# One transformer layer on one core: the prologue worked by halves of the first tile

## The reference

```python
mod = (silu(c) @ wmod).reshape(8, 6, 1, 128)       # sa, ca, ga, sb, cb, gb
h = layernorm(x) * (1 + ca) + sa
q, k, v = einsum('bsx,xAnh->Abnsh', h, w)          # 16 heads of 64; q += q_bias
emb = einsum('sf,fnh->nsh', sinusoids, positional) # relative positions
a = (q @ k.T + relative_causal(q @ emb.T)) * 64 ** -0.5
o = softmax(where(causal, a, -1e9)) @ v
x = x + ga * (o @ out_kernel + out_bias)
h = layernorm(x) * (1 + cb) + sb
x = x + gb * moe(h)      # 16 experts, argmax gate, 256 places each, 128 -> 512 -> 128
```

## Time and profile before

| | |
|---|---|
| median of 3 runs | 873.09 us (872.3 to 876.68) |
| the profiled execution's own time | 866.77 us |
| its span, first to last instruction | 864.9 us |
| PE busy in the span | 850.2 us, 98% |
| ACT, DVE, POOL busy | 84%, 76%, 62% |
| first x loads issued (ACT, SP); third load on ACT's queue | 0.72 us; 1.65 us |
| first score matmul starts | 17.86 us after the span's start |
| steps 0, 1, 2 last | 10.38, 13.09, 12.38 us |
| mean granted TensorE clock | 0.996 of full speed |

### The profile page before, as it was taken

How to read it: one execution, slowest core, us unless ns; L and a number is a source line. 1 busy time by engine, 2 the same in 40 slices (tenths; PEclk the granted TensorE clock), 3 DMA queues, 4 the chain that set the end, 5 groups by cost and what they waited for, 6 DMA issues and landing times.

```text
span 864.9 us, 17642 instructions
## 1 busy us (share of the span) xinstructions
PE 850.2 (98%) x5584; PEld 683.2 (79%) x5584; DVE 659.1 (76%) x2041; ACT 726.7 (84%) x2014; POOL 539.6 (62%) x797
## 2 busy tenths in 40 slices
PE   8999999999999999999999999999999999999996
PEld 6778777787777887778877788777887777877996
DVE  5878778887878778777878688777878767877574
ACT  5988889888888888888889888888988898885663
POOL 3655565666657766766576765776567755673465
PEclk9999999999999999999999999999999999999999
DMA  8000990000000100000000000000000000006781
GB/s 296 2 1 2 234 230 14 13 20 19 14 13 1 38 2 13 13 19 19 13 13 2 28 1 13 13 11 12 13 14 7 18 13 11 4 17 195 252 262 41
DMA packets 25468, 41.41 MB, mean 48 GB/s; under 512 B 3318, under 2 KB 17511, under 8 KB 24992
## 3 DMA queue, kind: packets, MB, share of 16 engines
q1 hardware_dynamic: 21728, 33.60, 13.1%
q0 software_dynamic: 3072, 5.94, 1.9%
q10 hardware_dynamic: 576, 0.75, 0.3%
HBM read 25.93 MB, written 16.82 MB: 49 GB/s over the span
## 4 chain that ended last, share of the span: by engine, by line
PE 92%; DVE 1%; DMA 1%; ACT 1%; issue 1%; POOL 0%; POOLq 0%; SPq 0%; DVEq 0%
PE bank L906 23%; PE bank L939 17%; PE bank L867 16%; PE bank L919 16%; PE bank L946 5%; PE bank L891 5%; PE bank L903 3%; PE bank L1206 3%; PE bank L1181 2%; DMA x<-xbuf 1%; ACT prob L640 0%; PE bank L1172 0%; PE bank L850 0%; PE bank L954 0%; PE bank L975 0%
## 5 line engine op out<-in xcount | busy, mean ns | idle before, releaser
L468 POOL TENSOR_SCALAR prob<-prob,rsum 128x128 f32<-128x128 f32 x508 | 263.0, 536 | 226.1 <-DVE rsum L1341 220.9
L640 ACT ACTIVATE prob<-srow,nmax 128x512 f32<-128x512 f32 (+3 forms) x512 | 285.9, 559 | 56.5 <-DVE nmax L1329 55.1
L1329 DVE CUSTOM_DVE_ANT_0 srow<-bank,consts 128x512 f32<-128x512 f32 (+3 forms) x512 | 247.0, 489 | 50.5 <-issue 38.5
L919 PE MATMUL bank<-consts,prob 128*128 128x128 f32 x1280 | 201.7, 272 | 0.4 <-ACT pt L649 0.4
L919 PEld LDWEIGHTS bank<-consts,prob 128*128 128x128 f32 x1280 | 158.1, 141 | 23.7 <-ACT pt L649 1.7
L649 ACT ACTIVATE pt<-bank 128x384 f32<-128x384 f32 x318 | 157.0, 498 | 10.6 <-PE bank L919 10.5
L1346 DVE SCALAR_TENSOR_TENSOR qx<-bank,qbias,consts 128x512 f32<-128x512 f32 x128 | 96.0, 750 | 72.9 <-PE bank L867 70.3
L939 PE MATMUL bank<-pt,v 128*64 128x512 f32 x1008 | 149.6, 439 | 0.2
L906 PE MATMUL bank<-khi,qhi 128*128 128x512 f32 (+2 forms) x384 | 140.4, 366 | 0.6 <-DVE nmax L1329 0.4
L461 POOL TENSOR_TENSOR qlo<-qx,qhi 128x384 fp32r<-128x384 f32 x128 | 129.3, 1010 | 13.8 <-ACT qhi L605 8.3
L906 PE MATMUL bank<-khi,qlo 128*128 128x512 f32 (+2 forms) x384 | 130.2, 339 | 0.0
(11 more groups left out here) (229 smaller groups left out, 1420.5 us busy)
## 6 DMA issues: line engine op xcount, KB each, us to landing
xbuf<-fill SPq DMA_DIRECT2D x4, 1540.0 KB, 24.0
x<-xbuf SPq DMA_DIRECT2D x13, 385.0 KB, 4.4
raw<-in_w SPq DMA_DIRECT2D x16, 256.0 KB, 10.1
prob<-in_w SPq DMA_DIRECT2D x16, 256.0 KB, 4.6
h2T<-in_xt SPq DMA_DIRECT2D x8, 256.0 KB, 2.7
out<-row SPq DMA_DIRECT2D x8, 256.0 KB, 2.3
x<-in_x SPq DMA_DIRECT2D x1, 1792.0 KB, 12.7
modb<-mod_rows SPq DMA_DIRECT2D x1, 1536.0 KB, 7.3
```

The lines of the kernel that those rows point to most:

```text
L468: end = gp.tensor_scalar(part, part, rsum[:, par, 4 * h + q:4 * h + q + 1], 1.0, ALU.mult, ALU.mult)
L640: act.activation(prob[:, par, h, QOFF[q]:QOFF[q] + P * (q + 1)], srow[:, k % 4, 0:P * (q + 1)], ACT.Exp, bias=nmax[:, par, k:k + 1], scale ...
L919: last = pe.transpose(out[:, n * P:(n + 1) * P], prob[:, par, h, QOFF[q] + k * P:QOFF[q] + (k + 1) * P], ident)
L1329: dve.tensor_tensor_reduce(out=srow[:, k % 4, 0:w], in0=scb[k % 2][:, 0:w], in1=mask[:, S - w:S], scale=-1.0, scalar=BIG, op0=ALU.add, op1 ...
```

## The change

- **Loads.** The two halves of the first x tile count on semaphores of their own. On ACT's queue the modulation weights go ahead of pair 0's weights; on SP's the table of query factors (`consts`) goes ahead of the sinusoids. The load of all other x is cut into batch 1 and the rest, which comes after the output weights.
- **First tile.** Statistics, root, x-hat and transposes are done for row tiles 2 and 3 first, then for 0 and 1. The first modulation columns are read by ACT. Modulation is computed twice, to fp32 by DVE and straight to the high part by ACT, half by half. The low parts of pair 0's weights move from DVE to POOL, and half of the sinusoids' low part too.
- **First products.** Keys come first, and the six products that need no low part of the input are mixed with those that do. The second modulation columns and rows come after them. The low part of the last query tile is made by DVE, that of the others by POOL.
- **First values.** The first four value tiles, and the one of step 1, are one plain fp32 matmul each, from `hn` and the raw weights. The split of the value weights moves from the prologue (high part on ACT, low part on POOL) to POOL in step 1.
- **Tables and casts.** The tables of pairs 1 to 3 move into step 0, those of pairs 4 to 7 into step 1. The casts of the weights of pairs 1 to 3 move from ACT to POOL.
- **Batch 1.** Its statistics move from block 0 of step 1 to blocks 6 and 7 of step 0, its x-hat from step 1 to blocks 0 and 1 of step 2. The copy of the modulation rows moves from step 1 to block 5 of step 0.
- **Idle matmuls.** 36 of 128 columns become 10 of 512; 20, 8 and 6 others are gone, 4 are new.

```diff
-    into = scb[1] if a0 == 0 else trb[i]
+    into = (scb[1] if a0 == 0 else trb[0], opb)[i]
...
-    sp.dma_start(h2T[HD:P, :], ktab_d).then_inc(s["ktab"], 16)
...
+    sp.dma_start(h2T[HD:P, :], ktab_d).then_inc(s["ktab"], 16)
...
-    sp.dma_start(x[:, QT:TILES, :], x_d[:, QT:TILES, :]).then_inc(s["x1"], 16)
+    sp.dma_start(x[:, QT:2 * QT, :], x_d[:, QT:2 * QT, :]).then_inc(s["x1"], 16)
...
+    sp.dma_start(x[:, 2 * QT:TILES, :], x_d[:, 2 * QT:TILES, :]).then_inc(s["xr"], 16)
...
-    root(0, 1, True)
+    gp.wait_ge(s["va0"], 1)
+    gp.tensor_tensor(rstd[:, 0, 2:QT], vare[:, 0, 2:QT], mhalf[:, 2:QT], ALU.pow).then_inc(s["rs0"], 1)
+    gp.wait_ge(s["va1"], 1)
+    gp.tensor_tensor(rstd[:, 0, 0:2], vare[:, 0, 0:2], mhalf[:, 0:2], ALU.pow).then_inc(s["rs1"], 1)
+    heads = lambda t: t[:, 0, 0:2 * P].rearrange("p (h c) -> p h c", h=2)[:, :, 0:HD]
+    gp.wait_ge(s["fhi"], 1)
+    gp.tensor_tensor(heads(wlo), wall[:, 0, 0:P].rearrange("p (h d) -> p h d", h=2), heads(whi),
+                     ALU.subtract).then_inc(s["flp"], 1)
+    gp.wait_ge(s["fhi"], 2)
+    gp.tensor_tensor(wlo[:, 0, 2 * P:3 * P], wall[:, 0, P:2 * P], whi[:, 0, 2 * P:3 * P], ALU.subtract)\
+        .then_inc(s["flp"], 1)
+    def high_w(a0, a1):
+        for h in range(2):
+            gp.tensor_copy(whi[q_cols(a0, a1, h)], wall[q_raw(a0, a1, h)]).then_inc(s["whp"], 1)
+        gp.tensor_copy(whi[:, a0:a1, 2 * P:3 * P], wall[:, a0:a1, P:2 * P]).then_inc(s["whp"], 1)
...
-    def low_wv():
+    def split_wv():
...
+        gp.wait_ge(s["w_v"], 16)
+        gp.tensor_copy(wvhi[:, :], wv).then_inc(s["wv"], 1)
...
-            low_q(j, 1)
+            if j > 0:
+                low_q(j, 1)
+            if first and a == 1:
+                split_wv()
...
+    waits(gp, ("kt", 2), ("flp", 2))
+    gp.tensor_tensor(klo[HD:P, 1, :], h2T[HD:P, :], khi[HD:P, 1, :], ALU.subtract).then_inc(s["klp"], 1)
+    waits(gp, ("klp", 1), ("qh", 1))
+    gp.tensor_tensor(qlo[:, 0, 0:2 * P], qx[:, 0, P:3 * P], qhi[:, 0, 0:2 * P], ALU.subtract)\
+        .then_inc(s["ql"], 1)
+    gp.wait_ge(s["wall1"], 16)
+    high_w(1, 4)
+    low_q(0, 1)
...
-    low_q(0, 0)
-    low_wk(1, 4, 3)
-    low_wv()
+    low_wk(1, 4, "whp", 3)
...
-    act.dma_start(x[:, 2:QT, :], x_d[:, 2:QT, :]).then_inc(s["x0"], 16)
-    act.dma_start(wall[:, 0:1, :], wall_d[:, 0:1, :]).then_inc(s["wall0"], 16)
+    act.dma_start(x[:, 2:QT, :], x_d[:, 2:QT, :]).then_inc(s["x0b"], 16)
...
+    act.dma_start(wall[:, 0:1, :], wall_d[:, 0:1, :]).then_inc(s["wall0"], 16)
...
-    bias_g(0, 1, 2)
+    act.wait_ge(s["mod_mm"], 1)
+    act.activation(modT[:, 0, :], bank[0][:, 0:B], ACT.Copy).then_inc(s["modT"], 1)
+    act.activation(modT[:, 1, :], bank[0][:, B:2 * B], ACT.Copy, bias=1.0).then_inc(s["modT"], 1)
+    def first_high():
+        act.wait_ge(s["t_x0"], 1)
+        act.wait_ge(s["modT"], 2)
+        act.activation(vhi[:, 2 * P:S], opb[:, 2 * P:S], ACT.Identity, bias=modT[:, 0, 0:1],
+                       scale=modT[:, 1, 0:1]).then_inc(s["vh0"], 1)
+        act.wait_ge(s["hn0"], 1)
+        act.activation(vhi[:, 0:2 * P], prb[0][:, 0:2 * P], ACT.Identity, bias=modT[:, 0, 0:1],
+                       scale=modT[:, 1, 0:1]).then_inc(s["vhi"], 1)
...
+        if k == 1:
+            high_g(1, 4, 3, "whi")
...
-            bias_g(1, PAIRS, 4)
-        if k == 3:
-            high_g(4, PAIRS, 5, "whi")
-        if k == 4:
-            act.wait_ge(s["wall2"], 16)
+            bias_g(1, 4, 4)
...
+        if k == 3:
+            high_g(4, PAIRS, 5, "whi")
+        if k == 4:
+            bias_g(4, PAIRS, 6)
+        if k == 5:
+            act.wait_ge(s["wall2"], 16)
...
+    first_high()
+    bias_g(0, 1, 2)
...
-    act.wait_ge(s["modT"], 2)
-    normed(0, opb)
-    high(0)
-    act.wait_ge(s["wall1"], 16)
-    high_wq(1, 4, 0)
-    high_wq(1, 4, 1)
-    high_wk(1, 4)
-    high_wv()
+    evac_k(0, 0, opb)
...
-    evac_k(0, 0)
-    evac_k(0, 1)
-    high_g(1, 4, 3, "whi")
+    evac_k(0, 1, opb)
...
-    pe.wait_ge(s["zero"], 2)
-    idle(36)
+    def idle_wide(n):
+        for _ in range(n):
+            pe.matmul(prb[0][:, :].rearrange("p (t c) -> p t c", t=QT), ones16[:, :],
+                      ones16[:, None, :].to_broadcast([P, QT, P]), start=True, stop=True)
+    pe.wait_ge(s["zero"], 1)
+    idle_wide(10)
...
-    pe.wait_ge(s["small"], 16)
-    b_table(0, 1)
...
-    idle(20)
...
-    turn_x(0, opb)
+    pe.wait_ge(s["xn0"], 1)
+    for q in (2, 3):
+        last = pe.transpose(opb[:, q * P:(q + 1) * P], xn[:, q, :], ident)
+    last.then_inc(s["t_x0"], 1)
+    pe.wait_ge(s["xn"], 1)
+    for q in (0, 1):
+        last = pe.transpose(prb[0][:, q * P:(q + 1) * P], xn[:, q, :], ident)
+    last.then_inc(s["t_x"], 1)
+    pe.wait_ge(s["small"], 16)
+    b_table(0, 1)
+    idle(4, trb[0])
+    def first_products():
+        k_of = lambda w, x_, i: pe.matmul(opb[:, :], w[:, 0, 2 * P:3 * P], x_, start=(i == 0), stop=(i == 2))
+        q_of = lambda h, w, x_, i: pe.matmul(prb[h][:, :], w[:, 0, h * P:(h + 1) * P], x_,
+                                             start=(i == 0), stop=(i == 2))
+        pe.wait_ge(s["fhi"], 3)
+        pe.wait_ge(s["flp"], 2)
+        pe.wait_ge(s["flo"], 1)
+        pe.wait_ge(s["hn"], 1)
+        pe.wait_ge(s["vhi"], 1)
+        k_of(whi, vhi[:, :], 0)
+        k_of(wlo, vhi[:, :], 1)
+        q_of(0, whi, vhi[:, :], 0)
+        pe.wait_ge(s["vlo"], 1)
+        k_of(whi, vlo[:, :], 2).then_inc(s["kp"], 1)
+        q_of(0, wlo, vhi[:, :], 1)
+        q_of(0, whi, vlo[:, :], 2).then_inc(s["qp"], 1)
+        pe.wait_ge(s["bias"], 2)
+        q_of(1, whi, vhi[:, :], 0)
+        q_of(1, wlo, vhi[:, :], 1)
+        q_of(1, whi, vlo[:, :], 2).then_inc(s["qp"], 1)
+    first_products()
...
-    idle(8)
...
+    def plain_v(out, g, t):
+        pe.matmul(out[:, :], hn[:, t * P:(t + 1) * P], wv[:, g * S:(g + 1) * S], start=True, stop=True)\
+            .then_inc(s["vp"], 1)
...
-        if k % QT == 0:
+        if j == 0 and k == 0:
+            pe.wait_ge(s["ql0"], 1)
+        elif k % QT == 0 or (j == 0 and k == 1):
...
-        if k == 2:
-            pe.wait_ge(s["modT"], 3)
-            w_table(4, PAIRS)
+        if k == 0:
+            pe.wait_ge(s["wall1"], 16)
+            w_table(1, 4)
+        if k == 1:
+            b_table(1, 4)
...
-            pe.wait_ge(s["wv"], 2)
+            pe.wait_ge(s["w_v"], 16)
...
-            pe.wait_ge(s["whi"], 5)
-            pe.wait_ge(s["wlo"], 2)
+            pe.wait_ge(s["modR"], 1)
...
-            project_v(V_INTO[k - 4], *V_FIRST[k - 4])
+            plain_v(V_INTO[k - 4], *V_FIRST[k - 4])
+    def second_step(k):
+        if k == 1:
+            pe.wait_ge(s["wall2"], 16)
+            pe.wait_ge(s["ve"], 1)
+            w_table(4, PAIRS)
+        if k == 2:
+            pe.wait_ge(s["bias"], 3)
+            b_table(4, PAIRS)
...
-                project_v(prb[1], *V_OF[a][1:])
+                if first and a == 2:
+                    pe.wait_ge(s["wv"], 2)
+                if first and a == 1:
+                    plain_v(prb[1], *V_OF[a][1:])
+                else:
+                    project_v(prb[1], *V_OF[a][1:])
+            if first and a == 1:
+                second_step(k)
...
-    pe.wait_ge(s["fhi"], 3)
-    pe.wait_ge(s["flo"], 3)
-    project_q(0, None, 0, 0)
-    project_q(0, None, 0, 1)
-    project_k(0, None, 0)
-    pe.wait_ge(s["wall1"], 16)
-    w_table(1, 4)
-    pe.wait_ge(s["wall2"], 16)
-    b_table(1, PAIRS)
-    pe.wait_ge(s["hn"], 1)
-    idle(6, opb)
...
+    dve.memset(ones16[:, :], 1.0).then_inc(s["zero"], 1)
...
-    dve.memset(ones16[:, :], 1.0).then_inc(s["zero"], 1)
...
-    dve.wait_ge(s["x0"], 32)
...
+    def first_stats(q0, landed, done, moments, ready):
+        dve.wait_ge(s[landed], 16)
+        for q in (q0, q0 + 1):
+            end = stats_of(0, q, x_of(0, q))
+        end.then_inc(s[done], 1)
+        dve.wait_ge(s[done], 1)
+        for q in (q0, q0 + 1):
+            end = dve.bn_aggr(mom[:, 0, q, :], stats[:, 0, q, :])
+        end.then_inc(s[moments], 1)
+        dve.wait_ge(s[moments], 1)
+        dve.tensor_scalar(vare[:, 0, q0:q0 + 2], mom[:, 0, q0:q0 + 2, 1], EPS, None, ALU.add)\
+            .then_inc(s[ready], 1)
+    def first_xhat(q0, ready, done):
+        dve.wait_ge(s[ready], 1)
+        for q in (q0, q0 + 1):
+            end = dve.tensor_scalar(xn[:, q, :], x_of(0, q), mom[:, 0, q, 0:1], rstd[:, 0, q:q + 1],
+                                    ALU.subtract, ALU.mult)
+        end.then_inc(s[done], 1)
+    first_stats(2, "x0b", "st0", "rst0", "va0")
+    first_stats(0, "x0", "st1", "rst1", "va1")
+    dve.wait_ge(s["e_silu"], 1)
...
-    dve.wait_ge(s["fhi"], 1)
-    heads = lambda t: t[:, 0, 0:2 * P].rearrange("p (h c) -> p h c", h=2)[:, :, 0:HD]
-    dve.tensor_tensor(heads(wlo), wall[:, 0, 0:P].rearrange("p (h d) -> p h d", h=2), heads(whi),
-                      ALU.subtract).then_inc(s["flo"], 1)
-    dve.wait_ge(s["fhi"], 2)
...
-    xhat1(0)
```

(69 more changed lines are left out.)

83 lines of the change are left out of this document (41 added, 42 removed).

## The result

The changed kernel took 877.53 us (median of 20 runs, 874.9 to 880.12), the kernel before 873.20 us beside it (20 runs, 871.94 to 876.96). The ratio is 1.0043, with a 95% interval of 1.0033 to 1.0053.

What follows compares the result with a forecast made beforehand. PE, busy for 98% of an 864.9 us span, was taken as the bound. Start -3.8, step 0 +2.75, step 1 -0.2, step 2 +0.2 sum to -1.05: 873.09 becomes 872.0 us; own range 870.5 to 873.5, whole 867.8 to 875.2.

Steps and rivals of the forecast that it cites:

- The start of the first scores: Prologue: first scores at 14.1 us instead of 17.86, -3.8 us, ends -5.3 and -2.0.
- the other branch: Prologue, beside PE's products and modulation: query evacuation, high part and low parts of keys and query, arriving at 13.9 us.
- the low clock lasts: Third rival: all nine products and modulation at clock 0.50, start 15.9, sum +0.8, 873.9 us; chance 0.13.
- Step 0, first half: First to fifth block: third maximum waits behind the table's cast and low part, fifth block at +5.15, so +1.55 us.
- Step 0, second half: Plain value tiles +0.76 and statistics with aggregates +0.66, instead of a wait of 0.25: +1.2 us.
- a wait that was there: End of step 0: a wait of 0.25 us before the change, set against the half's added costs.
- Step 1: Statistics go, tables, biases and one plain tile come (1.75 us): -0.2 us, ends -0.5 and +0.9.
- Loses its wait for the statistics: Step 1: ACT gets 0.6 + 0.18 us more on 11.85 busy, but no longer waits for the statistics.
- Step 2: Two pairs of x-hats delay the third maximum: +0.2 us, ends 0 and +0.8.
- 1.4 of 1.3 free: Step 2: the x-hats delay the third maximum by 1.4 us where 1.3 is free, giving +0.2.
- POOL's casts: Rival: POOL's casts hold the projection of pair 1, beside DVE done at 23.0, +3.0, 875.0 us; chance 0.15.
- count in full: Rival: the start's gain counts in full, step 0 costs only +0.8 to +1, total 867.8 to 869.6 us; chance 0.22.

Runs made afterwards that it cites:

- the filled prologue: Changed kernel with more 512-column multiplications of ones in the prologue (twelve instead of ten, more behind the table, modulation and transposes); ratio 1.0018 to the kernel before.
- columns later: Changed kernel with the low table part of pairs 1 to 3 and the late modulation columns moved later in step 0; ratio 1.0031 to the kernel before.
- statistics later: Changed kernel with batch 1's statistics and aggregate back at the start of step 1; ratio 1.0043 to the kernel before.
- the kernel before, filled: Kernel before with 41 instead of 20 multiplications of ones between the modulation's first part and the transposes; ratio 0.9994 to the kernel before.

## Why the prediction was wrong

*The start of the first scores* (-3.8, range -5.3 to -2.0; measured -2.55). Statistics, roots, x-hats, modulation and low part came as worked out (10.34 against 10.3); the x-hats took 1.53 beside POOL, where I had put 1.11 + 0.8, and a root of two columns 0.73, where I had taken 1.05. The step that failed is "I take the lower clock for the first three or four products and the full one after". All nine ran at 0.50, until 14.1 us, and the filled prologue showed its price, 1.95 us. It also showed that the other branch, which I had at 13.9, is done by 13.36. I had counted the ones-matmuls that the change takes out of PE's prologue and had the rival "the low clock lasts" for it, at 0.13. That was too little: the only row I had of the lower clock followed one idle stretch of 1.37 us. In the changed kernel the fall came 3.8 us earlier, behind three waits of 0.26 to 0.53 us (1.15 in all) between small matmuls.

*Step 0, first half* (+1.55; measured +1.58). Right in size and in chain: "columns later" took out 0.98 of it, and the fifth block came at +5.19 against the +5.15 worked out.

*Step 0, second half* (+1.2; measured +3.71). Here the sum broke, by two terms that it put at nothing. The second fall of the clock is 1.63: I had priced the 1.8 us wait of PE only as a wait, not as something behind which the clock can fall. The held base offsets are 0.93: I had counted DVE's instructions between the seventh maximum and the low keys, but not this one, since it took 0.17 before. I did not ask what it would stand beside, and there it had missed POOL's query part by 0.02 us. The two terms that I had are about right: the statistics and aggregate 0.55 for 0.66, and what remains without them, 7.47 against 6.77, is 0.70 for the four plain value tiles, priced at 0.76. (In that trace one takes 0.85 us, 22.38 to 23.23, against 3 x 0.23: 0.15 more each, 0.6 in all.) But the 0.25 that I took off for "a wait that was there" had nothing under it: in the kernel before the last matmuls ahead of step 1 start 0.23 to 0.24 us apart, and the earlier trace rows has PE busy for all of the 6.77.

*Step 1* (-0.2; measured +0.79). "Loses its wait for the statistics" was no gain: put back at the start of step 1, they made it 0.02 us longer (13.47 to 13.49). And the split on POOL, which I had called hidden by POOL's slack, costs 0.44: it delays the division and lengthens VectorE's largest operation, and half of TensorE's wait ahead of the weighted values goes with it. The other 0.4 us I did not take apart. TensorE's added tables and value tile are the likeliest, not the shown cause: without the split PE is busy for 13.12 of 13.49 us, against 11.96 of 13.09 before.

*Step 2* (+0.2; measured +1.20). "1.4 of 1.3 free" was the mis-sized term. The x-hats ahead of the second and third maximum take 1.36 us, and of these 1.10 came through; in step 1 they cost nothing. So the room was 0.3 us, not 1.3. The 1.3 were a sum of slack over the step, while the delay falls on these two maxima.

*The rivals.* POOL's casts did not hold the projection of pair 1: POOL was done at 19.04, and PE began it at 21.51. The start did not count in full, and that rival's far end was wrongly added: a start of -5.3 with +0.8 for step 0 gives -4.5 and 868.6 us, not -5.3 and 867.8. The low clock lasted, as the third rival said, but its 873.9 had only the first fall. Of my three signs of being wrong (step 0 below 11.5 us, scores before 12.8, a wait for POOL's low weights) none came; the first two could only have shown a better result than forecast.

Together: -2.55 + 1.58 + 3.71 + 0.79 + 1.20 = 4.73. By separate edits, the clock is 3.6 of what was paid (1.95 in the prologue, 1.63 in step 0), the table's wait 1.0, the held base offsets 0.9, the x-hats 1.1, the split 0.4 and the statistics 0.55. By difference at the full clock, the rest of the first half is 0.6, the plain tiles 0.7, the rest of step 1 0.4. That is 9.25 us, against the 4.5 (17.86 to 13.36) that the start gains at the full clock: 4.75 where 4.73 was measured. Three of these terms are what was left over in their stages, so that the sum closes proves nothing more. The sizes also go with the order of the edits: with the base offsets still held, the statistics were worth 1.37 us, of which I put about 0.2 down to a shorter low clock.

## What to carry to other kernels

A wait of TensorE in a short or thin stretch can cost twice: as itself and as a fall of the granted clock behind it, so an edit that thins out TensorE's work ahead of a dense stretch is to be priced at both clocks, and multiplications of ones in its idle time may be worth as much as the edit (here 3.6 us by the traces, 2.3 by the medians). They do not rule the fall out: single executions of the filled kernels still had a lower clock. Work that is moved into an in-order queue is to be placed by what stands behind it there: the same operations cost 1.1 us ahead of two maxima that TensorE waited for, and nothing behind the sixth and seventh maximum of the step ahead. And a short VectorE operation can cost as much as what is left of a GpSimd one beside it, as the base offsets did; copies from a matmul bank were not held.

## What the runs showed of the hardware

- The low clock of the prologue is not the same from execution to execution of one instruction stream. The changed kernel had 0.50 from 7.3 to 14.1 us; "statistics later", with the same prologue, from 8.9 to 19.2, and its first scores came 1.19 us later, 0.95 of it behind the products. In "columns later", the same once more, the clock rose only at 13.9. The Trainium skill, TensorE: Matmul & The Clock Gate, Part 1, calls the count of slow multiplications at a kernel's start run-variable; these traces agree. In the profiled executions of the filled prologues (eight variants of the changed kernel and the kernel before, filled) it never fell back to 0.50 between the first rise, at 4.2 to 6.9 us, and the experts at the end.
- A single wait of PE in a thin stretch can be followed by a fall. In the changed kernel PE idled 1.79 us up to 20.50, and the clock was at 0.50 from 20.97 to 24.39. With that gap filled, with a gap of 0.79 us, or with the same 1.79 us behind a filled prologue it stayed at 1.00 (the first and the last in one traced execution each).
- VectorE's operation on 16 columns took 0.16 to 0.18 us with GpSimd idle, 0.95 to 0.97 beside its subtraction of 384 columns, 0.79 and 0.80 beside its cast of 1024. Three copies of 8 columns from a matmul bank took 0.16 us each beside GpSimd's subtraction of weights (17.03 to 17.34 in the changed kernel). The other way round, GpSimd's cast of 512 columns took 1.61 or 1.62 us beside VectorE's subtraction of 1024 columns, 0.61 without it.
- The weight load of pair 0, 224 KB, lands at different times: ScalarE's cast of it started at 4.9 to 5.5 us in ten of the fourteen traces, at 6.2 to 6.5 in three and at 7.3 in one. Only the last moved the first scores, by 0.77 us.
